# The last stage of a gated convolution and mixture-of-experts kernel, fed and scaled in another way

## The reference

```
t    = layer_norm(x, eps 1e-6)                                  # over channels
xn   = norm_a * layer_norm(t, 1e-5) + norm_b
left = (xn @ Wl + bl) * sigmoid(xn @ Wlg + blg)
right= (xn @ Wr + br) * sigmoid(xn @ Wrg + brg)
gate = sigmoid(xn @ Wog + bog)
mix  = einsum('bkjd,bkid->bijd', left, right) / 384             # per channel, 384 x 384 x 384
x    = x + ((on_a * layer_norm(mix) + on_b) * gate) @ Wo + bo
y    = layer_norm(x)                                            # the tokens, 147456 of them
logits = y @ gate_w.T + gate_b                                  # 64 experts
probs  = softmax(logits over the tokens)
per expert: the 8 tokens of highest probability, pooled by it,
            through a two-layer gelu network of that expert (weight1, weight2),
            added back at those tokens, times their probabilities
```

## Time and profile before

| | |
|---|---|
| median of 3 runs | 3089.35 us (3086.25 to 3095.03) |
| the profiled execution's own time | 3078.97 us |
| its span | 3077.0 us |
| stage 1, stage 2, stage 3 and end (about) | 0 to 1120, 1120 to 1847, 1880 to 2950, to 3077 us |
| busy in 1950 to 2900 us: PE, DVE, ACT, POOL | 693.14, 735.21, 759.29, 796.74 us of 950 |
| DMA there | 304 GB/s, 86% of the engines' time |

### The profile page before, as it was taken

The page is one execution under the profiler, slowest core; times in us unless marked ns, Lnnn a source line. Parts: engine busy times, 40 slices in busy tenths (PEclk is TensorE's granted clock), DMA queues, the critical chain, the costliest instruction groups (busy, mean ns, idle before and its releaser), DMA issues.

```text
span 3077.0 us, 66113 instructions
## 1 busy us (share of the span) xinstructions
PE 2588.5 (84%) x14998; PEld 2145.9 (70%) x15070; DVE 2428.7 (79%) x4824; ACT 2363.5 (77%) x4284; POOL 1889.3 (61%) x2343
## 2 busy tenths in 40 slices
PE   7999999999999989989998984777777777777735
PEld 6888888888888878888988983555555555555523
DVE  6777777777777769999999996778777787787862
ACT  6888888888888877887878872888778787787850
POOL 8888888888888860000000003888788887887842
PEclk9999999999999999999999996999999999999967
DMA  5777777777777769999999985888888888888836
GB/s 199 270 267 268 267 270 273 270 269 269 267 268 268 270 256 318 333 327 325 343 330 325 332 295 185 301 309 307 297 300 309 303 299 298 309 309 297 303 139 202
DMA packets 281154, 873.00 MB, mean 284 GB/s; under 512 B 29223, under 2 KB 81602, under 8 KB 281122
## 3 DMA queue, kind: packets, MB, share of 16 engines
q1 hardware_dynamic: 272322, 855.31, 77.2%
q10 hardware_dynamic: 8448, 16.78, 1.6%
q0 software_dynamic: 352, 0.53, 0.2%
HBM read 492.97 MB, written 379.52 MB: 284 GB/s over the span
## 4 chain that ended last, share of the span: by engine, by line
PE 43%; DMA 17%; issue 14%; POOL 12%; DVE 5%; ACT 4%; SPq 2%; POOLq 1%; ACTq 0%; another core or an unknown queue 0%; DVEq 0%
PE banks L1267 32%; DMA arena<-left_d 11%; POOL rs L693 5%; DMA statrow<-stat_d 5%; POOL arena L664 4%; PE banks L1256 4%; PE banks L1335 3%; ACT arena L809 2%; PE banks L1301 1%; ACT work L879 1%; DVE left_parts L1006 1%; PE banks L1326 1%; PE banks L1336 1%; SPq L475 1%; DVE arena L1014 1%
## 5 line engine op out<-in xcount | busy, mean ns | idle before, releaser
L1267 PE MATMUL banks<-x_parts,w_parts 128*128 128x512 f32 x4320 | 1068.3, 399 | 0.8 <-POOL x_parts L626 0.8
L1267 PEld LDWEIGHTS banks<-x_parts,w_parts 128*128 128x128 f32 x4320 | 791.9, 189 | 162.9 <-POOL x_parts L626 1.2
L1301 PE MATMUL banks<-left_parts,right_parts 128*128 128x384 f32 x3456 | 629.3, 341 | 67.2 <-ACT arena L810 56.8
L1301 PEld LDWEIGHTS banks<-left_parts,right_parts 128*128 128x128 f32 x3456 | 606.2, 191 | 90.5 <-issue 86.0
L957 DVE SCALAR_TENSOR_TENSOR arena<-banks,cols,arena 128x512 f32<-128x512 f32 x576 | 406.6, 747 | 255.7 <-ACT arena L775 252.3
L879 ACT ACTIVATE work<-arena,nmr,rs 128x128 f32<-128x128 f32 x1152 | 458.9, 482 | 151.9 <-POOL nmr L695 145.5
L659 POOL COPY rcol<-late 128x8 f32 (+1 forms) x144 | 28.4, 197 | 722.3 <-ACT late L825 722.3
L664 POOL TENSOR_TENSOR arena<-arena,work 128x512 f32<-128x512 f32 x288 | 359.7, 1270 | 163.1 <-DVE arena L1063 161.9
L1335 PE MATMUL banks<-wo_sb,arena 128*128 128x128 f32 x2304 | 413.3, 309 | 0.1
L1335 PEld LDWEIGHTS banks<-wo_sb,arena 128*128 128x128 f32 x2304 | 373.6, 200 | 29.4 <-issue 1.8
L626 POOL TENSOR_TENSOR x_parts<-xn,x_parts 128x512 fp32r<-128x512 f32 x288 | 372.2, 1292 | 6.6 <-ACT x_parts L763 6.6
(11 more groups left out here) (177 smaller groups left out, 4459.5 us busy)
## 6 DMA issues: line engine op xcount, KB each, us to landing
arena<-in_x_dram SPq DMA_DIRECT2D x144, 512.0 KB, 3.4
left_d<-arena SPq DMA_DIRECT2D x144, 512.0 KB, 2.6
right_d<-arena SPq DMA_DIRECT2D x144, 512.0 KB, 3.4
gate_d<-arena SPq DMA_DIRECT2D x144, 512.0 KB, 4.2
arena<-right_d SPq DMA_DIRECT2D x128, 576.0 KB, 5.8
arena<-left_d SPq DMA_DIRECT2D x128, 576.0 KB, 6.8
mixed_d<-arena SPq DMA_DIRECT2D x128, 576.0 KB, 4.2
work<-mixed_d SPq DMA_DIRECT2D x144, 512.0 KB, 4.2
```

Of the source, the lines that this page charges most:

```text
L1267: last = nc.tensor.matmul(ps[2 + k][:, :], w_parts[:, wq, k], x_parts[:, xq, b, c], start=((wq, xq) == TERMS[0]), stop=((wq, xq) == TERMS[ ...
L1301: last = nc.tensor.matmul(ps[NT * b + t][:, 0:GRID], lr_parts[RIGHT][:, rq, b, k, t * P:(t + 1) * P], lr_parts[LEFT][:, lq, b, k], start=( ...
```

## The change

It has six parts, all but one in stage 3.

1. `statrow` has four places in place of two. SP loads the rows of step s+3 in pass s, before the other loads; the wait is for the projection of step s-1. For that the loops of SP and PE run over four steps (`quads`).
2. The weight pieces: each cut issues one load of 0.5 MB, so there are 28 cuts in the loop of ACT where there were seven, and four loads behind it where there were two.
3. ACT computes the exponentials right behind `scale_rest`, ahead of `normalise`. Their sum goes straight to `csum`; POOL's copy of it and the buffer `esum` are gone.
4. The gating weights are centred over the channels once, at the start (three small DVE operations, for which the PE transpose of the weights waits). So the mean need not be taken off the tokens: `normalise` is a product with `rs` alone, and `minus` (DVE) and `nmr` (POOL) are gone.
5. POOL copies the kept values and places once for two steps.
6. `exact`, `exact_lo` and `exact_p` lie in `yt`; this frees the room for `statrow`.

```diff
+def quads(engine, steps, body, drain=0):
+    last = steps // 4 - 1
+    body(0)
+    with engine.Fori(1, last) as j:
+        body(j)
+    for j in range(last, steps // 4 + drain):
+        body(j)
...
-        statrow = sb("statrow", [P, 2, 2, CHUNK], BF16)
+        statrow = sb("statrow", [P, 4, 2, CHUNK], BF16)
...
-            def load_parts(i, b):
-                s = 2 * i + b
-                sp.wait_ge(s_z3, mark(2, s - 2, 2))
+            def load_parts(j, r):
+                s = 4 * j + r
+                if not isinstance(j, int) or j > 0:
+                    sp.wait_ge(s_z3, mark(2, s - 4, 2))
...
+            def stage3(j):
+                for r in range(4):
+                    if in_range4(j, r, 3, STEPS):
+                        load_parts(*shifted4(j, r, 3))
+                    if in_range4(j, r, 2, STEPS):
+                        load_mixed(*halves_of(*shifted4(j, r, 2)))
+                    if in_range4(j, r, -1, STEPS):
+                        store_result(*halves_of(*shifted4(j, r, -1)))
+                    if in_range4(j, r, 1, STEPS):
+                        load_x3(*halves_of(*shifted4(j, r, 1)))
...
-            def keep_sum(i, b):
-                s = 2 * i + b
-                pool.wait_ge(s_e3, mark(1, s, 1))
-                nc.gpsimd.tensor_copy(csum[:, bass.ds(s, 1)], esum[:, b]).then_inc(s_qs, 1)
+            def keep(i):
+                pool.wait_ge(s_m3, mark(2, 2 * i + 1, 2))
+                nc.gpsimd.tensor_copy(cand[:, bass.ds(2 * i, 2), :], mx[:, :, :])
+                nc.gpsimd.tensor_copy(cidx[:, bass.ds(2 * i, 2), :], ix[:, :, :]).then_inc(s_q3, 1)
...
-                pool.wait_ge(s_n3, mark(2, s, 1))
-                nc.gpsimd.tensor_tensor(nmr[:, b], minus[:, b], rs[:, b], ALU.mult).then_inc(s_n3, 1)
...
             def load_w1(n):
-                for j in range(2 * n, 2 * n + 2):
-                    act.dma_start(w1_sb[:, j], w1_view[j]).then_inc(s_w1, 16)
+                j, first = n // 2, BANDS // 2 * (n % 2)
+                some = slice(first, first + BANDS // 2)
+                act.dma_start(w1_sb[:, j, some], w1_view[j, :, some]).then_inc(s_w1, 16)
...
-                act.wait_ge(s_qs, mark(1, s - 2, 1))
                 nc.scalar.activation(expo[:, :], ps[6 + b][:, :], ACT.Exp, bias=negmax[:, b],
-                                     accum_out=esum[:, b]).then_inc(s_e3, 1)
+                                     accum_out=csum[:, bass.ds(s, 1)]).then_inc(s_e3, 1)
...
-                        last = nc.scalar.activation(ys[:, b, h, c], summed[:, b, h, c], ACT.Identity,
-                                                    bias=nmr[:, b, k:k + 1], scale=rs[:, b, k:k + 1])
+                        last = nc.scalar.activation(ys[:, b, h, c], summed[:, b, h, c], ACT.Copy, scale=rs[:, b, k:k + 1])
...
-            cuts = [lambda n=n: load_w1(n) for n in range(WLOADS - 1)]
+            cuts = [lambda n=n: load_w1(n) for n in range(4 * (WLOADS - 1))]
...
+            link(nc.vector.tensor_reduce(gsum[:, :], gate_nat[:, :], AXX, ALU.add))
+            link(nc.vector.tensor_scalar(gsum[:, :], gsum[:, :], 1.0 / DIM, None, ALU.mult))
+            nc.vector.tensor_scalar(gate_nat[:, :], gate_nat[:, :], gsum[:, :], None, ALU.subtract).then_inc(s_gmean, 1)
             dve.wait_ge(s_gtp, 1)
...
-                nc.vector.tensor_scalar(over_tiles(minus[:, b]), bn[:, b, :, :, MEAN], -1.0, None, ALU.mult)
...
             pe.wait_ge(s_const, 16 * N_CONST)
+            pe.wait_ge(s_gmean, 1)
...
-                    nc.tensor.matmul(ps[h][:, :], coef[:, 0, :], statrow[:, b, h, :], start=True, stop=True).then_inc(s_c3, 1)
+                    nc.tensor.matmul(ps[h][:, :], coef[:, 0, :], statrow[:, r, h, :], start=True, stop=True).then_inc(s_c3, 1)
```

More of the change, by code:

```diff
@@ L86, in pairs, with shifted4, in_range4, halves_of @@
         body(i)
+def quads(engine, steps, body, drain=0):
[5 more added lines that the diff above has]
+        body(j)
+def shifted4(j, r, k):
+    return j + (r + k) // 4, (r + k) % 4
+def in_range4(j, r, k, steps):
+    return not isinstance(j, int) or 0 <= 4 * j + r + k < steps
+def halves_of(j, r):
+    return 2 * j + r // 2, r % 2
 def build(nc, x, norm_a, norm_b, Wl, bl, Wr, br, Wlg, blg, Wrg, brg, Wog, bog, on_a, on_b, Wo, bo,
@@ L235, in build @@
         rs = sb("rs", [P, 2, 2 * TILES])
-        minus = sb("minus", [P, 2, 2 * TILES])
-        nmr = sb("nmr", [P, 2, 2 * TILES])
         mhalf = sb("mhalf", [P, 2 * TILES])
@@ L351, in build @@
         s_x3 = [sem(f"s_x3{b}") for b in range(2)]
-        s_sin = [sem(f"s_sin{b}") for b in range(2)]
+        s_sin = [sem(f"s_sin{r}") for r in range(4)]
         s_rc = sem("s_rc")
@@ L537, in _ @@
             sp.wait_ge(s_stst, 16 * 2 * PARTS)
-            load_parts(0, 0)
-            load_parts(0, 1)
-            pairs(sp, STEPS, stage3, drain=1)
+            for r in range(3):
+                load_parts(0, r)
+            quads(sp, STEPS, stage3, drain=1)
             w2_view = weight2[:, 0:HIDDEN, :].rearrange("(g j) (p c) n -> j p g (c n)", g=BANDS, c=HC)
@@ L886, in stage3 @@
                         scale_rest(i, b)
+                    if in_range(i, b, -4, STEPS):
+                        exponentials(*shifted(i, b, -4))
                     if in_range(i, b, -1, STEPS):
@@ L900, in _ @@
                 act.wait_ge(s_ost[b], 16 * (STEPS // 2))
-            load_w1(WLOADS - 1)
+            for n in range(4 * (WLOADS - 1), 4 * WLOADS):
+                load_w1(n)
             act.wait_ge(s_nm, 1)
@@ L923, in _ @@
                 dve.sem_inc(s_, 2 * n)
[L925 removed]
+            for s_, n in ((s_lo2, 2), (s_rstd, 1), (s_xhp, 1), (s_lo, 2), (s_rc, 1), (s_g3, 2), (s_ra, 1), (s_n3, 1), (s_k3, 1), (s_q3, 1)):
                 dve.sem_inc(s_, 2 * n)
@@ L1335, in project @@
                         nc.tensor.matmul(ps[2 + h][:, tok], gated[:, b, h, tok], wo_sb[:, :], start=True, stop=False)
-                        last = nc.tensor.matmul(ps[2 + h][:, tok], statrow[:, b, h, tok], coef[:, 1, :], start=False, stop=True)
+                        last = nc.tensor.matmul(ps[2 + h][:, tok], statrow[:, r, h, tok], coef[:, 1, :], start=False, stop=True)
                     last.then_inc(s_z3, 1)
@@ L1354, in logits, with stage3 @@
                                      start=True, stop=True).then_inc(s_l3, 1)
-            def stage3(i):
-                for b in range(2):
-                    if in_range(i, b, 1, STEPS):
-                        outer(*shifted(i, b, 1))
-                    if in_range(i, b, 0, STEPS):
-                        project(i, b)
-                    if in_range(i, b, -3, STEPS):
-                        logits(*shifted(i, b, -3))
-                    if in_range(i, b, -2, STEPS):
-                        transposes3(*shifted(i, b, -2))
+            def stage3(j):
+                for r in range(4):
+                    if in_range4(j, r, 1, STEPS):
+                        outer(*shifted4(j, r, 1))
+                    if in_range4(j, r, 0, STEPS):
+                        project(j, r)
+                    if in_range4(j, r, -3, STEPS):
+                        logits(*halves_of(*shifted4(j, r, -3)))
+                    if in_range4(j, r, -2, STEPS):
+                        transposes3(*halves_of(*shifted4(j, r, -2)))
             pe.wait_ge(s_rtc, NT * NT)
```

62 lines of the change are left out of this document (22 added, 40 removed).

## The result

The changed kernel takes **2895.86 us** (median of 4 runs, 2891.38 to 2896.39), the kernel before 3092.19 us (4 runs beside it, 3086.25 to 3099.24): ratio 0.9361, 95% interval 0.9338 to 0.9384. The forecast was 2985 us with a range of 2925 to 3045. The direction was right; the gain is 196 us where 104 were forecast, and the time lies outside the range. The profiled execution took 2896.19 us, its span is 2894.4.

A forecast was written before the change was run, and what follows sets the result against it. Stage 3 was taken as bound by the latency of the small statistics-row load, then by the DMA rate. Profiled 3078.97 - 98 - 9 + 3 = 2975 us, plus 10.4 to the median, gave 2985 us, range 2925 to 3045.

The forecast's parts named there:

- What bounds the kernel now: Stage 3: the statistics rows' load latency, 4.42 us of a turn, queued behind 512 KB transfers; afterwards the DMA rate.
- 353 x 0.96 = 339 GB/s: Stage 3 DMA rate after the change, scaled from 304 GB/s at share 0.86: 6.63 us a step, -98 us.
- The floors: Stage 3 pass without waits: POOL 5.83 us, DVE 5.64 us, both below the DMA's 6.63 us.
- Pieces at zero: Weight loads of 0.5 MB at ACT's cuts in stage 3: no gain or loss booked; 11 us if cover went.
- rival D: First use of any load behind a cut: each piece stalls 5.09 us like a whole load, 3128 us; chance 0.03.
- Exponentials first and `normalise` at zero: ACT's pass in stage 3: earlier exponentials and bias-free `normalise` (0 to 0.94 us less per step) booked as no gain.
- Copies at zero: POOL's copies once for two steps in stage 3: zero, at worst 0.5 us every second pass (36 us).
- Start: Before the first stage: larger `statrow` memset +1.8 us, centring the gating weights about +1.5 us, together +3 us.
- A: Stage 3 DMA rate rises with load to 375 GB/s or more; 6.1 us a step, 2912 us; chance 0.17.
- B: Stage 3 in-order queue leaves request gaps: DMA share near 0.91, 321 GB/s, 3036 us; chance 0.2.
- C: ACT's 29 loops in stage 3 make it wait for code fetches, +86 us, about 3070 us; chance 0.04.
- E: Stage 3 rows were not the bound; step stays near 7.3 us, 3085 us; chance 0.03.

The follow-up runs named there:

- two places: Changed kernel with two places for the statistics rows, loaded at the end of SP's pass, all else kept: 3157.45 us, ratio 1.0247.
- fewer bytes: Changed kernel loading x for only half of the tiles from the third step of stage 3 on: 2865.7 us, ratio 0.9272.
- lighter engines: Changed kernel with POOL's power replaced by a product and half of DVE's statistics left out, all transfers kept: 2917.27 us, ratio 0.9448.
- part 1 alone: Kernel before with only four places for the statistics rows, and the room made for them in `yt`: 3011.1 us, ratio 0.9753.
- part 4 undone: Changed kernel with `minus`, `nmr` and the bias in `normalise` back, gating weights not centred: 2923.87 us, ratio 0.9464.
- the rows by ACT: Kernel before with the statistics rows' load issued by ACT at the head of its pass, not by SP: 3189.36 us, ratio 1.0334.
- PE kept busy: Kernel before with the 0.5 MB weight pieces and five extra PE products ahead of the wait for the rows: 3098.4 us, ratio 1.0032.
- the best version: Changed kernel with 4 MB of weights issued between stages 2 and 3, memset and centring moved behind stage 1: 2882.7 us, ratio to before 0.9334.
- part 2 undone: Changed kernel with weights loaded again as 1 MB pairs at seven cuts: 2902.95 us, ratio 0.9384.

## Why the prediction was off

The miss is 2985 - 2896 = 89 us: 69 in the steps of stage 3 (98 + 9 = 107 forecast, 176 measured), about 9 in what lies ahead of it and behind it (3 lost forecast, 6 gained, of which the first store's 4.4 are no more than the spread named above), and 10 from the correction to the median, which the changed kernel doesn't need (its profiled execution, 2896.19, is its median).

- **What bounds the kernel now**: right. With two places the rows bind, with four PE waits for them no more, and the DMA is next: fewer bytes make the kernel faster, lighter engines do not. But the reason given for the 4.42 us was half right. They are not the place in SP's queue: from ACT's queue the rows take 4.32 us.
- **The step that failed: "353 x 0.96 = 339 GB/s".** Measured are 362 GB/s at a share of 0.98, so 369 for a full share. The factor 0.96 cost 2%, the 353 another 4.5%. At 362 GB/s the forecast's bytes give 2.247 / 0.362 = 6.21 us a step where it had 6.63; measured are 6.17. Scaling by the share took it for granted that the engines move as much per busy time in a fuller queue. The runs show that they moved more: 353 at a share of 0.79 (two places), 356 at 0.91 (part 1 alone), 364 at 0.97 (part 4 undone), 369 at 0.98. The share is not all of it: 348 at 0.79 with the rows by ACT, 360 at 0.83 with PE kept busy, 355 at 0.94 with half of x. Why the rate per busy time rises stays open. Stage 2's 351, with another mix of transfers, was taken at 0.94, so it was no check of a full queue.
- **The cap of the Trainium skill** (DMA: Bandwidth & Descriptors, Specifications) that the prediction set aside, 358 GB/s of HBM for a core, would have given 806 us for the stretch in place of 852. By 362 GB/s it would be 288.68 / 362 = 797. The measurement is 1% above the skill's figure, and the figure was a better term than the forecast's own. Another page of the Trainium skill (Perfetto Trace Analysis, Roofline) allows a core that is alone more than that share, and the trace agrees, by that 1% over 750 us.
- **The floors**: POOL's 5.83 us is 5.93 by the run with fewer bytes. Right that it is below the DMA; the distance is 0.24 us, not 0.8.
- **Pieces at zero**: right for the changed kernel (undoing them makes no clear difference), wrong as to why. Alone they make the kernel before 61 us slower. The forecast's rival D named the place and took the price from the load's stall; what costs is PE's clock, and in the changed kernel, whose clock is 1.00, the cost is gone. Two counts beside it are off without effect: there are 14 issues more, not 21 (28 single loads for 7 pairs), and a piece comes every 5 passes, not every 2 or 3. A part that is harmless behind one edit was not harmless without it.
- **Exponentials first and `normalise` at zero**: wrong. Part 1 alone ends at 6.95 us, above the forecast's 6.63, since the loop through the exponentials was overlooked as a floor, 6.77 us a step by its round: PE's 107.0 us of waits for them in the earlier trace rows stood there and was booked as covered by the rows. With the rows gone, it was next. Both parts together, with the small ones, are worth 3011 - 2896 = 115 us.
- **Copies at zero**: no run undoes part 5. A step of 6.17 us at a DMA share of 0.98 leaves little room for 0.5 us in every second pass; that is argued, not tested.
- **Start**: 4.1 us for 3; moving it away again was part of the best version.
- **The rivals.** A came nearest (2912 us and 6.1 us a step), though by a rate of 369 and not over 375. By the forecast's own sign for A, over 370 GB/s, it did not occur either. B and C did not occur: the share is 0.98, and with 8 loops on ACT in place of 29 (part 2 undone) the kernel is not faster. E is refuted by part 1 alone.

## What to carry to other kernels

When a chain of waits is opened, look for the next chain before the next resource: list each wait that the old one covers, and take its loop's length as a floor beside the DMA and the engines. A DMA rate taken at a share of 0.86 and scaled up was 4.5% too low here for a full queue: take it as a lower bound, not as the middle of the range. And a loop that makes PE wait for a load can pay twice, once for the load and once for the clock, as this one did; there pieces of the same bytes cost 61 us, and products that only keep PE busy gave 56 back.

## What the runs showed of the hardware

- After a wait of 2.62 us in the loop, PE's granted clock was 0.67 in the stretch behind it, and the 28 products of a turn took 5.1 us where they take 3.3. Five idle products of 1.1 us in all, put into the wait, brought the mean clock from 0.90 to 0.99 and 56 us back.
- 28 loads of 0.5 MB disturbed the closed loop by 61 us; with 14 loads of 1 MB in pairs 7 of 100 turns were slow. With the loop open there is no clear difference.
- One core held 362 GB/s of mixed loads and stores for 750 us. With 188 us less work on POOL the rate was not higher, 353.
- An activation with one operand from a tensor less is 93 ns shorter (481 to 388 ns at `normalise`). The Trainium skill (ScalarE: Activation LUTs, What ACT_TABLE_LOAD costs) has just this price for such an operand.
